# Two heads of a pair in the two halves of TensorE's rows, and one key tile of values a step

## What is computed

```python
sup = relu(ctx @ W_fc.T + b_fc)                 # (8, 1601, 256)
ref = relu(layernorm(x) @ W_fc.T + b_fc)        # (8, 256, 256)
q = (ref @ W_q.T + b_q)                         # 16 heads of 16
k = (sup @ W_k.T + b_k)
p = softmax(einsum('bqhd,bkhd->bhqk', q, k) / 4)
attn = per head: (p @ sup) @ Wv_head.T          # values: sup @ Wv_head.T, 16 a head
x = x + ref + attn + b_v
x = x + shared_ffn(layernorm(x)) + top2_of_8_experts(layernorm(x))
```

## Time and profile before

| | |
|---|---|
| median of 3 runs (lowest to highest) | 1279.07 us (1276.35 to 1281.3) |
| profiled execution, its span | 1282.98 us, 1281.2 us |
| TensorE busy | 1217.5 us, 95% |
| its weight loads | 914.9 us, 71% |
| VectorE, ScalarE, GpSimd busy | 62%, 54%, 29% |
| mean granted TensorE clock | 0.976 of full speed |
| scores L403 / transposed scores L424 / values L436 | 1024 / 832 / 3328 matmuls |

### The profile page before, as it was taken

One profiled execution on the slowest core, in us unless ns is written; L12 is line 12 of the kernel. 1 busy time (PEld: TensorE's weight loads), 2 busy tenths in 40 slices (PEclk: granted clock), 3 DMA queues, 4 the chain that ended last, 5 costly groups with the idle time before them and its releaser, 6 DMA issues. The chain is left out here.

```text
span 1281.2 us, 23263 instructions
## 1 busy us (share of the span) xinstructions
PE 1217.5 (95%) x8550; PEld 914.9 (71%) x8550; DVE 791.7 (62%) x1669; ACT 688.9 (54%) x954; POOL 371.5 (29%) x282
## 2 busy tenths in 40 slices
PE   6899999999999999999999999999999969999994
PEld 5767777777777777777777777766546867888884
DVE  5266676767777777777777676777835433444442
ACT  4436666666656666666666666656663222222221
POOL 4403223322332342233223222311102540223332
PEclk8879999999999999999999999999998998999998
DMA  6766576678768666776866667674615858633333
GB/s 194 228 164 178 175 209 169 184 202 214 204 220 240 182 179 206 215 198 226 229 191 175 190 177 188 197 179 93 155 59 219 327 199 279 196 56 55 51 55 90
DMA packets 164510, 228.88 MB, mean 179 GB/s; under 512 B 65568, under 2 KB 134568, under 8 KB 164336
## 3 DMA queue, kind: packets, MB, share of 16 engines
q1 hardware_dynamic: 149952, 194.80, 53.1%
q0 software_dynamic: 9216, 16.46, 6.0%
q10 hardware_dynamic: 5232, 16.13, 3.5%
HBM read 133.56 MB, written 95.68 MB: 179 GB/s over the span
## 5 line engine op out<-in xcount | busy, mean ns | idle before, releaser
L628 DVE TENSOR_REDUCE mx<-side 128x1 f32<-128x400 f32 (+1 forms) x1024 | 534.8, 569 | 143.3 <-PE side L403 134.8
L495 ACT ACTIVATE prob<-st 128x1024 f32<-128x1024 f32 (+1 forms) x416 | 412.5, 1022 | 183.6 <-PE st L424 181.7
L403 PE MATMUL side<-kst,qst 96*128 96x400 f32 (+1 forms) x1024 | 331.1, 383 | 7.0 <-DVE mx L628 3.2
L403 PEld LDWEIGHTS side<-kst,qst 96*128 96x128 f32 x1024 | 190.0, 190 | 118.8 <-issue 38.1
L424 PE MATMUL st<-qst,kst 97*128 97x512 f32 (+1 forms) x832 | 266.0, 403 | 5.3 <-ACT prob L495 3.3
L436 PE MATMUL acc<-prob,v 128*32 128x256 f32 (+1 forms) x3328 | 206.8, 384 | 0.0
L424 PEld LDWEIGHTS st<-qst,kst 97*128 97x128 f32 (+1 forms) x832 | 148.2, 186 | 18.8 <-ACT prob L495 9.0
L436 PEld LDWEIGHTS acc<-prob,v 128*32 128x32 f32 (+1 forms) x3328 | 95.4, 110 | 78.8 <-issue 21.2
L660 POOL TENSOR_TENSOR clo<-raw,chi 128x768 fp32r<-128x768 f32 (+1 forms) x32 | 60.8, 1901 | 299.1 <-ACT chi L526 299.1
L666 POOL TENSOR_TENSOR flo<-fc,fhi 128x768 fp32r<-128x768 f32 (+1 forms) x32 | 61.1, 1909 | 204.6 <-ACT fhi L539 204.6
L1550 POOL DMA_INDIRECT token_sums<-yg,rows_of x39 | 60.9, 1561 | 163.1 <-DMA token_sums<-yg,rows_of 101.6
(11 more groups left out here) (195 smaller groups left out, 1677.0 us busy)
## 6 DMA issues: line engine op xcount, KB each, us to landing
kst<-parts_at SPq DMA_DIRECT2D x90, 400.2 KB, 6.0
parts_at<-parts SPq DMA_DIRECT2D x48, 384.0 KB, 6.8
wall<-w_at ACTq DMA_DIRECT2D x10, 1536.0 KB, 9.2
w_at<-piece_hi SPq DMA_DIRECT2D x27, 512.0 KB, 6.7
w_at<-piece SPq DMA_DIRECT2D x27, 512.0 KB, 5.8
v<-v_at SPq DMA_DIRECT2D x32, 408.0 KB
raw<-ctx_t SPq DMA_DIRECT2D x24, 384.0 KB, 5.3
piece<-gate_up SPq DMA_DIRECT2D x18, 512.0 KB, 4.9
```

Source lines behind the costliest of these rows:

```text
L403: pe.matmul(side[u.bank][:, 0:w], t.qst[0:96, pair, col * P:(col + 1) * P], t.kst[0:96, pair, o:o + w], start=True, stop=True).then_inc(si ...
L495: act.activation(prob[0:rows, s, :], st[(KT * g + s) % 2][0:rows, :], ACT.Exp, scale=float(DH) ** -0.5).then_inc(exp_done, 1)
L628: dve.tensor_reduce(mx[:, p % 2, hq, r:r + 1], side[u.bank][:, 0:RANGES[r][1]], AX.X, ALU.max)\
```

## The change

The two heads of a pair move into the two halves of the array's rows: the first into rows 0 to 47, the second into rows 64 to 111, with the row of ones and of maxima at 48 and 112. A score then takes 48 rows and one head's own queries; `qst` is half as wide, holds no zeros and isn't cleared. Consecutive scores alternate between the halves. The transposed scores of a step become four matmuls of 256 columns instead of two of 512, the two heads of a pair one after the other and into different banks. Keys are loaded by six DMAs a group instead of three, the row of ones and the row of maxima by two instead of one. In `STEP` one tile of values stands in each step, tile n two steps behind its scores, and tiles 11 and 12 in the first two steps of the next phase. In the expert part `turn_x(0)` moves ahead of the three loads of weights on ScalarE.

```diff
 STEP = [
-    ["p 0", "0 xturn 0", "p 1", "1 stat"],
-    ["S", "v 0", "S", "0 xturn 1"],
-    ["S"],
-    ["S", "S", "v 1", "S", "chi", "S"],
-    ["S", "S", "1 norm", "prev 8", "prev 9", "prev 10", "prev 11", "prev 12", "accout", "S", "0 xchi"],
-    ["S", "S", "f 0", "S", "S"],
-    ["S", "f 1", "S", "S"],
-    ["fhi", "S", "out", "V 0", "V 1", "S"],
-    ["S", "S", "0 xfc"],
-    ["S", "S"],
-    ["1 xp", "S", "1 xres", "V 2", "V 3", "V 4", "V 5", "tm", "S"],
-    ["S", "S"],
-    ["S", "S", "V 6", "V 7", "S", "S", "S"],
+    ["p 0", "0 xturn 0", "p 1", "prev 11", "1 stat"],
+    ["S", "S", "v 0", "prev 12", "accout", "0 xturn 1"],
+    ["S", "S", "V 0"],
+    ["S", "S", "v 1", "chi", "V 1", "S", "S"],
+    ["S", "S", "1 norm", "V 2", "0 xchi"],
+    ["S", "S", "f 0", "V 3", "S", "S"],
+    ["S", "S", "f 1", "V 4", "S"],
+    ["fhi", "S", "S", "out", "V 5"],
+    ["S", "S", "0 xfc", "V 6"],
+    ["S", "S", "V 7"],
+    ["S", "1 xp", "1 xres", "V 8", "tm", "S"],
+    ["S", "S", "V 9"],
+    ["S", "S", "V 10", "S", "S", "S"],
 ]
...
-            pair, col = GP * g + hq // 4, hq % 4
-            pe.matmul(side[u.bank][:, 0:w], t.qst[0:96, pair, col * P:(col + 1) * P], t.kst[0:96, pair, o:o + w],
-                      start=True, stop=True).then_inc(side_full, 1)
+            pair, q, at = GP * g + hq // 4, hq // 2 % QT, HALF * (hq % 2)
+            pe.matmul(side[u.bank][:, 0:w], t.qst[at:at + PART_ROWS, pair, q * P:(q + 1) * P],
+                      t.kst[at:at + PART_ROWS, pair, o:o + w], start=True, stop=True).then_inc(side_full, 1)
...
             for i in range(GP):
-                mm = pe.matmul(into[0:rows, i * 2 * NQ:(i + 1) * 2 * NQ],
-                               t.kst[0:97, GP * g + i, s * P:s * P + rows],
-                               t.qst[0:97, GP * g + i, :], start=True, stop=True)
+                for j in range(2):
+                    at, end = HALF * j, HALF * j + PART_ROWS + 1
+                    mm = pe.matmul(into[0:rows, (GP * j + i) * NQ:(GP * j + i + 1) * NQ],
+                                   t.kst[at:end, GP * g + i, s * P:s * P + rows],
+                                   t.qst[at:end, GP * g + i, :], start=True, stop=True)
...
-                sp.dma_start(t.kst[32 * i:32 * i + 32, pairs, o:end].bitcast(F32),
-                             rows_of(parts_at, b, part)[:, pairs, o:end]).then_inc(s, 16)
+                for j in range(2):
+                    at = HALF * j + DH * i
+                    sp.dma_start(t.kst[at:at + DH, pairs, o:end].bitcast(F32),
+                                 rows_of(parts_at, b, part)[DH * j:DH * (j + 1), pairs, o:end]).then_inc(s, 16)
...
-            sp.dma_start(t.qst[96:97, GP * g:GP * (g + 1), :].rearrange("p a n -> p (a n)").bitcast(F32),
-                         mrow[:, :].bitcast(F32)).then_inc(row_in, 16)
+            for j in range(2):
+                at = HALF * j + PART_ROWS
+                sp.dma_start(t.qst[at:at + 1, GP * g:GP * (g + 1), :].rearrange("p a n -> p (a n)").bitcast(F32),
+                             mrow[j:GQ:2, :].bitcast(F32)).then_inc(row_in, 16)
...
-                dve.memset(t.qst[0:96, :, :].bitcast(F32), 0.0).then_inc(zero_done, 1)
...
+                turn_x(0)
+
                 for e, a in FIRST_LATE:
                     load_part(act, place(e), w_at, e, a, late_in)
-                turn_x(0)
```

More of the change, by code:

```diff
@@ L43 @@
 BANKS = 3
+HALF = P // 2
+PART_ROWS = 3 * DH
 def key_rows(kt):
@@ L436, in pe_values @@
                 mm = pe.matmul(acc[32 * j:32 * j + 32, 0:NQ], t.v[0:rows, g, kt, VS * j:VS * j + 32],
-                               prob[0:rows, kt, j * NQ:(j + 1) * NQ], start=(kt == 0), stop=(kt == KT - 1))
+                               prob[0:rows, kt, (GP * (j % 2) + j // 2) * NQ:(GP * (j % 2) + j // 2 + 1) * NQ],
+                               start=(kt == 0), stop=(kt == KT - 1))
             mm.then_inc(pv_done, 1)
@@ L789, in sp_load_queries @@
                 for j in range(2):
-                    r = 16 * j
-                    sp.dma_start(t.qst[32 * i + r:32 * i + r + 16, pairs, j * NQ:(j + 1) * NQ].bitcast(F32),
-                                 rows_of(q_at, b, part)[r:r + 16, pairs, :]).then_inc(qst_in[g], 16)
+                    at = HALF * j + DH * i
+                    sp.dma_start(t.qst[at:at + DH, pairs, :].bitcast(F32),
+                                 rows_of(q_at, b, part)[DH * j:DH * (j + 1), pairs, :]).then_inc(qst_in[g], 16)
         def sp_load_keys(sp, b, g, o, end, s):
@@ L875, in _ @@
                 sp.wait_ge(ones_done, 1)
-                sp.dma_start(t.kst[96:97, :, :].rearrange("p a n -> p (a n)").bitcast(F32), t.ones).then_inc(ones_in, 16)
+                for j in range(2):
+                    at = HALF * j + PART_ROWS
+                    sp.dma_start(t.kst[at:at + 1, :, :].rearrange("p a n -> p (a n)").bitcast(F32), t.ones)\
+                      .then_inc(ones_in, 16)
                 sp_load_chunk(sp, 1, 0, 1)
@@ L1237, in _ @@
                 batches(pe, body)
-                for kt in range(8, KT):
+                for kt in range(KT - 2, KT):
                     pe_values(pe, PHASES - 1, B - 1, GROUPS - 1, kt)
@@ L1921, in attend @@
         t.kst = sb("kst", [P, PAIRS, NK], F32R)
-        t.qst = sb("qst", [P, PAIRS, 2 * NQ], F32R)
+        t.qst = sb("qst", [P, PAIRS, NQ], F32R)
         t.v = sb("v", [P, GROUPS, KT, VW], F32)
```

15 lines of the change are left out of this document (7 added, 8 removed).

## The result

The changed kernel takes **1323.95 us** (median of four runs, 1312.97 to 1326.09), the kernel before 1280.18 on the same chip: ratio 1.031 (1.028 to 1.035), slower. Forecast was 1271. The profiled execution's span is 1324.3 where before had 1281.2, and its mean granted clock 0.952 where before had 0.976. The run of 1312.97 had the same mean clock as the kernel before, 0.976, and still took 33 us more, so the clock alone is not the loss. Of two later kernels some runs were longer at a lower granted clock; their times are medians of the others.

A forecast was written before the change was run, and what follows sets the result against it. TensorE was taken to bound the attention loop, with VectorE 7.5 us in hand. The terms +5 + 5 - 10 - 4 + 2 - 6 made -8 us, on the median's footing 1271 us, range 1185 to 1325.

The forecast's parts named there:

- (a): Scores in halves, attention loop: two run together in 0.183 us, 16 pairs save 2.93 us a phase; bounds 0 to -2.93.
- (b): Transposed scores, attention loop: four matmuls of 256 columns in pairs, 6.06 us a phase becomes 3.07, -2.99.
- Partial overlap: Rival for the halves: a pair takes 0.24 us instead of 0.183, phase 28.1, about 1307 us in all; chance 0.20.
- (c): Values one tile a step: 13 runs instead of 4, 9 x 0.335 = +3.0 us a phase; between +1.5 and +3.0.
- (d): Switches between halves and full array: 0.2 us at each of 7 stretches, +1.4 a phase; bounds 0 and +2.9.
- (e): TensorE's waits on VectorE and three banks in the loop: 2.85 us a phase, against 1.0 before.
- (f): Second DMA for the row of maxima, 0.66 us on SyncE: taken as nothing, bound 0.66 a phase.
- 27 phases x 0.2: Loop phases with projections: fourth kind's growth from 26.7 to 26.9 us applied to all 27, +5 us.
- the 0.8 of `norm`: Phases of the second kind: VectorE's `norm`, now beside one tile of values, costs about 0.8 us; 7 x 0.8 = +5.
- Clock, "no case": Attention loop: granted clock at 1.00 and TensorE's pauses under 1 us, so clock was dismissed as a rival.
- Phases 27 to 30: Attention phases without projections: from 22.9 us each to 20.4, 4 x -2.5 = -10 us.
- Experts: Expert part: `turn_x(0)` ahead of the weight loads removes TensorE's wait for first rows, -6 us; bounds 0 and -10.

The follow-up runs named there:

- the second run: Changed kernel with halves of 64 rows, the keys' filling rows written behind the prelude's loads and prelude scores kept at 48 rows: 1326.43 us, ratio 1.033.

## Why the prediction was wrong

By its own steps, in its order:

- **(a), (b) halves side by side**: right as a rate, too high as a sum. A pair lasts as long as one matmul, 0.35 for two scores; the quiet step is 1.20 for 1.19. Partial overlap, the rival with the Trainium skill's 3.07 of 4 behind it (TensorE: Matmul & The Clock Gate, Part 3), is out: two halves run at their full rate in this trace. But the forecast took all 16 pairs of scores. In `STEP` four scores of a phase stand alone (steps 6, 10, 10 and 12), and others wait for a bank without their partner: from 200 to 850 only 208 pairs of 353 start together. By the estimate above a phase streams 19.7 us, not 18.3; of the 5.9 some 4.4 came.
- **(c) runs of values**: right as a price (+3.1 measured for +3.0 with full rows; 0.34 in the trace of after). What the text didn't say: it is a price only while nothing else sets the step. With halves, five to nine fewer runs gave nothing back.
- **(d) halves against the full array**: 0.2 a stretch was right where values follow (0.19 in step 5). In and out between halves is 0.31 to 0.4, but no stretch of the fourth kind has halves on both sides. The high end, 2.9, would need both ways to be paid at all seven, and the way to the values is already in (c). The page cited there (TensorEngine Tiling (Array Packing), section Key Properties, of the Trainium skill) says that a change of tiling mode drains TensorE. The trace agrees: in the lines above every change from or to halves leaves 0.09 to 0.14.
- **(e) waits on VectorE and three banks**: right in place and nearly in size. The fourth score starts 0.59 behind its partner for 0.6; `v 0` 0.29 late (0.57, of which 0.183 streams and 0.10 is the switch) for 0.2; `tm` waits for the maximum, 0.38 of idle time for 0.6. The sign named for it, over 2 us a phase of load waits on `mx`, did not come: it is 1.3. The sum of 2.85 can't be read off one line; the edit with a fourth bank took back 0.9 of it.
- **(f) row of maxima**: put at nothing because no row showed how much was spare, and not nothing. Loads' waits on `mrow` went from 1.3 us to 4.4 between 200 and 900, the matmuls' from 0.2 to 2.1: 3 to 5 us.
- **The phase**: 27.3 in the window above, 27.4 in most phases of this kind, for 26.9. **The step that failed is the next one, "27 phases x 0.2"**: the fourth kind stood for all. On average over the loop the four kinds grew by 1.4, 1.3, 1.0 and 0.8, where 0.2, 1.0 (with `norm`), 0.2 and 0.2 were forecast, and the 27 phases together by 29.5 for 10. This is the largest part of the miss. Some of it has a name in the waits (mean of a phase in the two traces, from phase 4 on): in the second kind TensorE now waits 0.7 us for VectorE's `xparts` and 0.5 for GpSimd's `clo`, and before for neither; in the first its loads wait 0.4 for the row of maxima, before 0.1. The second kind didn't grow more than the first, which has no `norm`, so the 0.8 of `norm` isn't seen.
- **Clock, "no case"**: wrong, and no term of the sum. Its reason, pauses under 1 us, held: in the 5.4 us before the fall at 885.4 TensorE paused for 0.42 and 0.72 us. What had changed was that the full-array projections stopped and only halves of 48 and 49 rows and values were left. With 64 rows phases 27 to 30 took 9.5 less (8.1 in the second run). The last phase lost to it too: its twelve steps with transposed scores took 16.5 before (clock 0.90), 19.9 at a clock of 0.57 in the kernel after, and 12.7 at 1.00 in the run with the loads first. At full clock the -4 forecast for it would have been right.
- **Phases 27 to 30**: -10 forecast, +6.8 measured. 8 to 9.5 are the clock; at 1.00 the last two of them took 21.2 each on average, before 22.7, and 20.4 was the forecast. The rest is mostly in phase 27: with 64 rows and the clock at 1.00 nearly throughout it took 25.1, of which TensorE waits 3.5 for the first turned rows. (In the kernel after the half clock covers this wait: TensorE has no gap there.)
- **Prelude** +4.1 for +2, inside its bounds. **Experts** -6: nothing. The wait that was removed was real, and the next one was the store of `y` on the same crowded path, which the step never priced.

Sum of the misses in the span: 2 + 19.5 + 17 + 13 = 51, of which the clock is some 16 (9 in phases 27 and 28, 7 in the last). The range of 1185 to 1325 holds 1324 at its very edge, which is luck, since the sign was wrong; and that the fourth kind came within 0.5 is luck in part: 1.4 us too little streaming stood against 0.9 too much for switches and waits (27.4 - 19.7 = 7.7 for 8.6). Of the rivals none was it: it is the forecast's own mechanism with more waits in the other three kinds, plus a clock that no rival had. Neither of its signs of being wrong came (pairs 0.18 apart, phases under 25): none of them watched the other kinds of phase or the clock. Two of its sums are off a little: the terms listed under (e) make 2.8, and partial overlap makes 1309.

What stays open: the rest of what makes the first three kinds grow more than the fourth, above all the third; why 48 and 49 rows keep the clock at 0.50 so long, and why rows that hold only zeros in one operand help; and why the clock fell at 885.4 at all.

## What to carry to other kernels

Where matmuls are made shorter by using less of the array at a time, ask what their length had covered: here the ring of banks became the limit in many steps, the ring of exponentials stood close behind it once runs were joined or banks moved, and what one saved came back as a wait of the other. Count which matmuls really meet in the order of work, not how many there are. Price a change between halves and the full array like one to column strips, and count each change once. One kind of phase doesn't stand for the others. Before a wait is moved away, look for the next transfer on the same path and price that too, and ask of the granted clock what the engine will still do in the stretches where its full-array work ends.

## What was not expected of the hardware

- The granted clock stayed at 0.50 for 41 us with TensorE busy 41.00 of them, and for 136.5 us (136.24 busy) in the kernel whose heads follow each other in the same half. With all rows in use and the same order of steps it stayed at 1.00 through the same phases (93.7 us), and with the halves filled to 64 rows at 0.98 (88.7 us).
- Two halves of 48 rows run wholly side by side in rounded fp32, each with its own weight load: two scores in 0.35 us, the time of one.
- From halves to one full-array matmul and back is 0.31 to 0.4 us, about as much as from full rows to column strips and back (0.335); with column strips behind the full-array stretch it costs 0.19 on the way in.
